# Two adaLN feed-forward layers on one core: the sort before everything, three blocks of items by gathers, eight places for block outputs, weights split two blocks later

## The reference, cut to what matters

```python
def _L0_cond_ref(x, weight, adapter_ids):        # x (64, 32, 512), weight (8, 512, 512)
    w = weight[adapter_ids]
    return jnp.einsum('bsi,boi->bso', x, w)

h  = _L0_cond_ref(x, L0_cond_weight, itok_B_3_7)
x  = x + (h @ kernel + bias + delta_lora(h, gate) + h @ A_shared.T @ B_shared.T)
c  = gated_ffn_with_lora(x, itok_B_2_6)          # 1376 wide, silu(gate) * up, down
x  = x + (c @ W.T + b + routed_lora(c))          # the best of four ranks per token
```

## Time and profile before

| | us |
|---|---|
| median of 3 runs (709.83 to 710.42) | 710.22 |
| the profiled execution | 711.87 |
| its span | 709.9 |
| TensorE busy | 682.0 (96%) |
| TensorE weight loads busy | 567.9 (80%) |
| VectorE busy | 312.5 (44%) |
| ScalarE busy | 281.5 (40%) |
| POOL busy | 346.0 (49%) |

### The profile page before, as it was taken

The page is one execution under the profiler, slowest core; times in us unless marked ns, Lnnn a source line. Parts: engine busy times, 40 slices in busy tenths (PEclk is TensorE's granted clock), DMA queues, the critical chain, the costliest instruction groups (busy, mean ns, idle before and its releaser), DMA issues. The chain is left out here.

```text
span 709.9 us, 11120 instructions
## 1 busy us (share of the span) xinstructions
PE 682.0 (96%) x3388; PEld 567.9 (80%) x3388; DVE 312.5 (44%) x719; ACT 281.5 (40%) x606; POOL 346.0 (49%) x266
## 2 busy tenths in 40 slices
PE   5799999998999999999999999999999999989997
PEld 3678788886788888888888888888888888867775
DVE  3788677646522223622222642142462223244664
ACT  2675542213543333543333554343454433343210
POOL 0034400231788765587766488776558777300000
PEclk9999999999999999999999999999999999999999
DMA  8963561121245336345334335433434434100112
GB/s 301 372 251 138 190 223 60 37 76 46 87 158 172 112 106 238 102 141 154 123 119 145 97 116 164 143 113 102 153 110 141 148 113 132 51 1 0 60 63 116
DMA packets 32210, 91.80 MB, mean 129 GB/s; under 512 B 5312, under 2 KB 5440, under 8 KB 30624
## 3 DMA queue, kind: packets, MB, share of 16 engines
q1 hardware_dynamic: 21936, 61.05, 25.5%
q0 software_dynamic: 10080, 30.16, 12.8%
q10 hardware_dynamic: 144, 0.00, 0.0%
HBM read 81.23 MB, written 9.96 MB: 128 GB/s over the span
## 5 line engine op out<-in xcount | busy, mean ns | idle before, releaser
L570 POOL TENSOR_TENSOR gu_lo<-gu_raw,gu_hi 128x1024 fp32r<-128x1024 f32 x44 | 113.2, 2572 | 101.7 <-ACT gu_hi L649 101.6
L1242 DVE TENSOR_TENSOR act_f<-psU,silu 128x512 f32<-128x512 f32 x44 | 30.4, 692 | 181.5 <-ACT silu L809 181.5
L601 POOL DMA_INDIRECT ab<-in_ab,idx_tab x88 | 85.9, 976 | 20.8 <-issue 17.3
L809 ACT ACTIVATE silu<-psG 128x512 f32<-128x512 f32 x44 | 26.2, 596 | 147.5 <-PE psG L1360 147.4
L1353 PE MATMUL psG<-x_hi,gu_hi 128*128 128x512 f32 x176 | 72.3, 411 | 1.2 <-ACT silu L809 1.2
L1353 PE MATMUL psD<-act_hi,dn_hi 128*128 128x512 f32 x176 | 69.0, 392 | 0.0
L1354 PE MATMUL psD<-act_lo,dn_hi 128*128 128x512 f32 x176 | 69.0, 392 | 0.0
L1355 PE MATMUL psG<-x_hi,gu_lo 128*128 128x512 f32 x176 | 68.9, 392 | 0.0
L1353 PE MATMUL psU<-x_hi,gu_hi 128*128 128x512 f32 x176 | 68.9, 391 | 0.0
L1354 PE MATMUL psG<-x_lo,gu_hi 128*128 128x512 f32 x176 | 68.6, 390 | 0.0
L1355 PE MATMUL psD<-act_hi,dn_lo 128*128 128x512 f32 x176 | 68.6, 390 | 0.0
(11 more groups left out here) (324 smaller groups left out, 1613.3 us busy)
## 6 DMA issues: line engine op xcount, KB each, us to landing
gu_raw<-in_gu SPq DMA_DIRECT2D x44, 512.0 KB, 3.5
dn_raw<-in_dn SPq DMA_DIRECT2D x44, 256.0 KB, 4.2
cond_w_raw<-in_cond_w SPq DMA_DIRECT2D x8, 1024.0 KB, 6.9
x_all<-in_x_t SPq DMA_DIRECT2D x4, 1024.0 KB, 10.5
tok<-h_scratch SPq DMA_DIRECT2D x4, 1024.0 KB, 5.5
out_t<-x_all SPq DMA_DIRECT2D x16, 256.0 KB, 2.1
ab<-in_ab,idx_tab POOLq DMA_INDIRECT x88, 3.8
kraw<-in_kern SPq DMA_DIRECT2D x1, 1024.0 KB, 11.9
```

Of the source, the lines that this page charges most:

```text
L570: pool.tensor_tensor(dst, x, hi, ALU.subtract).then_inc(s, 1)
L601: pool.indirect_dma_start(ab[:, par, g, :], None, a["ab"], bass.IndirectOffsetOnAxis(idx_tab[:, NGT * t + g, fc:fc + 1], 0)).then_inc(S[f" ...
L809: act.activation(silu[:], psG[:], ACT.Silu).then_inc(S["silu_s"], 1)
L1242: dve.tensor_tensor(act_f[:], psU[:], silu[:], ALU.mult).then_inc(S["act_f_s"], 1)
```

## The change

The sort's table is cut in three and its first part (64 rows of the columns that the sort needs, 115 KB) is loaded first, on ACT's queue, and the rest of the early part behind `ids1`, also there. `shared` is loaded three times, to 96 partitions, so that hi and lo parts stand above each other: the fold is one product of 96 rows per quarter instead of three of 32, and moves behind the products of `perm`; VectorE's split of it moves behind `blk_w`. VectorE makes `idx_x`, rows of x for blocks 0 to 2, and POOL gathers them from HBM into the first three places of `h0`; TensorE transposes them (`turn_x`: 0 ahead of block 0, 1 inside it, 2 behind it), and ScalarE and VectorE split them out of PSUM (`high_xg`, `low_xg`). Only x(0) and x(1) are loaded before the first weight; x(2) and x(3) wait for `xg_sent`, and weights 1 and 2 follow. Weight 1 is split at b = 0, weight k at b = 2(k - 1), and weights 3 to 7 are loaded when `c_ps` reaches b - 4 of their split; `kraw` goes behind weight 4. Blocks 4 to 7 are evicted to four more places (`h0_far`, in the last slot of `w_hi`). VectorE's loop over the blocks changes as ScalarE's does, and `scatter_rows` stands ahead of `low_w0(0)`. The diff, cut to its core:

```diff
 CONST_W = {
-    "ident": P, "adapter_no": N_ADP, "adapter_eighth": N_COND, "before": ITEMS, "ones": P, "fours": ITEMS // BI,
-    "slot_no": SLOTS, "delta": RANK0, "item_no": P, "dummy": SLOTS, "quadrant": BI, "row_in_item": 1,
-    "own_group": GROUPS, "heads": ITEMS,
+    "adapter_eighth": N_COND, "before": ITEMS, "ones": P, "fours": ITEMS // BI, "slot_no": SLOTS, "item_no": P,
+    "adapter_no": N_ADP,
+    "ident": P, "quadrant": BI, "row_in_item": 1, "own_group": GROUPS, "heads": ITEMS, "dummy": SLOTS, "delta": RANK0,
...
+        h0_far = sb("h0_far", [P, RING, D], F32, at=w_at - slot_bytes)
+        X_BANK = (psX, psG, psT)
...
+        SPLIT_AT = {2 * (k - 1): k for k in range(1, N_COND)}
...
+        def is_far(b):
+            return RING <= b < 2 * RING
+        def spot(b):
+            return (h0_far if is_far(b) else h0)[:, b % RING, :]
+        def spot_free(eng, b):
+            if b >= 2 * RING:
+                eng.wait_ge(S[f"c_st{b % RING}"], 16 * (b // RING - 1))
...
@@ block.sync
             sp.dma_start(ids0[:], a["ids0"]).then_inc(S["ids0_in"], 16)
-            sp.dma_start(const[:, 0:CONST_EARLY], a["const"][:, 0:CONST_EARLY]).then_inc(S["const_in"], 16)
-            sp.dma_start(sh[:], a["shared"]).then_inc(S["shared_in"], 16)
-            for t in range(NTB):
+            for k in range(3):
+                sp.dma_start(sh[k * RANK0:k * RANK0 + RANK0], a["shared"]).then_inc(S["shared_in"], 16)
+            def load_x(t):
                 sp.dma_start(x_all[:, :, tokens_of(t)], a["x_t"][t].rearrange("p (c n) -> p c n", c=C)
                              ).then_inc(S["x_all_in"], 16)
+            load_x(0)
+            load_x(1)
             sp.wait_ge(S["order_ready"], 1)
-            for k in range(3):
-                load_w(k)
-            sp.dma_start(kraw[:], a["kern"]).then_inc(S["kraw_in"], 16)
-            sp.dma_start(gate_v[:], a["gate"]).then_inc(S["gate_in"], 16)
+            load_w(0)
+            sp.wait_ge(S["xg_sent"], 1)
+            load_x(2)
+            load_x(3)
+            load_w(1)
+            load_w(2)
             sp.wait_ge(S["kern_ps"], C)
             sp.wait_ge(S["blk_ready"], 1)
             sp.wait_ge(S["idx_ready"], 1)
-            for k in range(3, N_COND):
-                sp.wait_ge(S["w_hi_s"], split_w(k - 3))
-                load_w(k)
+            sp.wait_ge(S["xg_ps"], AHEAD)
+            for b, k in SPLIT_AT.items():
+                if k > 2:
+                    multiplied(sp, b - 4)
+                    load_w(k)
+                if k == 4:
+                    sp.dma_start(kraw[:], a["kern"]).then_inc(S["kraw_in"], 16)
+                    sp.dma_start(gate_v[:], a["gate"]).then_inc(S["gate_in"], 16)
...
@@ block.gpsimd
+            pool.wait_ge(S["idx_x_ready"], 1)
+            for b in range(AHEAD):
+                pool.indirect_dma_start(h0[:, b, :], None, a["x"], bass.IndirectOffsetOnAxis(idx_x[:, b:b + 1], 0)
+                                        ).then_inc(S[f"xg_in{b}"], 16)
+                if b == 1:
+                    pool.tensor_copy(sent[:], idx_x[:]).then_inc(S["xg_sent"], 1)
             pool.wait_ge(S["idx_ready"], 1)
...
@@ block.scalar
+            act.dma_start(const[0:ITEMS, 0:CONST_SORT], a["const"][0:ITEMS, 0:CONST_SORT]).then_inc(S["const_in"], 16)
             act.dma_start(ids1[:], a["ids1"]).then_inc(S["ids1_in"], 16)
+            act.dma_start(const[:, CONST_SORT:CONST_EARLY], a["const"][:, CONST_SORT:CONST_EARLY]
+                          ).then_inc(S["ends_in"], 16)
+            act.wait_ge(S["shared_in"], 48)
+            high(sh_r[:], sh[:], S["sh_hi_s"])
+            def high_xg(b):
+                act.wait_ge(S["xg_ps"], b + 1)
+                high(xs_hi[:, b].rearrange("p c j n -> p (c j n)"), X_BANK[b][:], S["xs_hi"], BI)
             folded(0)
             folded(1)
+            act.wait_ge(S["w_in0"], 16)
+            high_w0(0)
+            high_xg(0)
+            for c in range(1, C):
+                high_w0(c)
+            folded(2)
+            high_xg(1)
+            folded(3)
+            high_xg(2)
             act.wait_ge(S["item_ready"], 1)
-            cols = item_cols(act, 0), item_cols(act, 1)
-            folded(2)
-            folded(3)
             act.wait_ge(S["x_all_in"], 16 * NTB)
-            high_xs(0, cols[0])
-            high_xs(1, cols[1])
-            act.wait_ge(S["w_in0"], 16)
-            for c in range(C):
-                high(w_hi[:, 0, c * D:c * D + D], w_raw[:, 0, c * D:c * D + D], S["w_hi_s"])
-            high_xs(2)
-            high_w(1)
             for b in range(NBLK):
...
-                if b % W_EVERY == 0 and b // W_EVERY + 2 < N_COND:
-                    high_w(b // W_EVERY + 2)
+                if b in SPLIT_AT:
+                    high_w(SPLIT_AT[b])
...
@@ block.vector
+            then(dve.tensor_tensor(sel_g[:], psT[:, 0:AHEAD * BI].rearrange("p (b j) -> p b j", j=BI),
+                                   cst("quadrant").unsqueeze(1).broadcast_to([P, AHEAD, BI]), ALU.mult))
+            then(dve.tensor_reduce(row_x[:], sel_g[:], AX.X, ALU.add))
+            dve.tensor_scalar(idx_x[:], row_x[:], float(ITEM_T), cst("row_in_item"), ALU.mult, ALU.add
+                              ).then_inc(S["idx_x_ready"], 1)
+            def low_xg(b):
+                dve.wait_ge(S["xs_hi"], BI * (b + 1))
+                flat = [v[:, b].rearrange("p c j n -> p (c j n)") for v in (xs_hi, xs_lo)]
+                dve.tensor_tensor(flat[1], X_BANK[b][:], flat[0], ALU.subtract).then_inc(S["xs_lo"], BI)
+            scatter_rows()
+            low_w0(0)
+            low_xg(0)
+            for c in range(1, C):
+                low_w0(c)
+            low_xg(1)
+            low_xg(2)
+            keep_counts()
...
@@ block.tensor
+            pe.wait_ge(S["sh_lo_s"], 2)
+            for c in range(C):
+                pe.matmul(psD[:, c, :], sh_r[:, 0, c * P:c * P + P], sh_r[:, 1, :], start=True, stop=True
+                          ).then_inc(S["kern_ps"], 1)
+            def turn_x(b):
+                pe.wait_ge(S[f"xg_in{b}"], 16)
+                if b == 2:
+                    pe.wait_ge(S["idx_ready"], 1)
+                for c in range(C):
+                    mm = pe.transpose(X_BANK[b][:, c * P:c * P + P], h0[:, b, c * P:c * P + P], ident)
+                mm.then_inc(S["xg_ps"], 1)
...
                     mm = pe.matmul(ps, xh, w[1], start=False, stop=c == C - 1)
+                    if b == 0 and c == 1:
+                        turn_x(1)
                 mm.then_inc(S["c_ps"], 1)
             pe.wait_ge(S["blk_ready"], 1)
             e = adapter(0)
+            turn_x(0)
             for b in range(NBLK):
                 after = adapter(b + 1) if b + 1 < NBLK else None
                 cond(b, e)
+                if b == 0:
+                    turn_x(2)
                 e = after
```

More of the change, by code:

```diff
@@ L278, in two_layers @@
         sh_at = w_at + 6 * slot_bytes
-        sh = sb("shared", [RANK0, 2, D], F32, at=sh_at)
-        sh_lo = sb("shared_lo", [RANK0, 2, D], F32R, at=sh_at)
-        sh_hi = sb("shared_hi", [RANK0, 2, D], F32R, at=sh_at + 4 * 2 * D)
+        sh = sb("shared", [3 * RANK0, 2, D], F32, at=sh_at)
+        sh_r = sb("shared_r", [3 * RANK0, 2, D], F32R, at=sh_at + 4 * 2 * D)
         top["at"] = w_at + 5 * slot_bytes
@@ L289, in two_layers @@
         own = sb("own", [ITEMS, N_COND], F32)
+        sel_g = sb("sel_g", [P, AHEAD, BI], F32)
+        row_x = sb("row_x", [P, AHEAD], F32)
+        idx_x = sb("idx_x", [P, AHEAD], U32)
+        sent = sb("sent", [P, AHEAD], U32)
         slot = sb("slot", [ITEMS, 1], F32)
@@ L382, in two_layers @@
         a_rows = a["ab"].rearrange("n (k d) -> (n k) d", k=3)
-        names = """ids0_in const_in shared_in gate_in small_in ids1_in lora_a_in lora_b_in kraw_in late_in
+        names = """ids0_in const_in ends_in shared_in idx_x_ready xg_sent xg_in0 xg_in1 xg_in2 xg_ps gate_in small_in ids1_in lora_a_in lora_b_in kraw_in late_in
             w_in0 w_in1 w_in2 w_in3 w_in4 w_in5 w_in6 w_in7
@@ L389, in two_layers @@
             kern_ps kfold_s kern_f kern_hi kern_lo aeff_ps beff_ps aeff_done beff_even beff_odd
-            w_hi_s w_lo_s xs_hi xs_lo c_ps c_out0 c_out1 c_st0 c_st1 c_st2 c_st3
+            w_hi_s w_lo_s xs_hi xs_lo c_ps c_out0 c_out1 c_st0 c_st1 c_st2 c_st3 c_far0 c_far1 c_far2 c_far3
             wf_hi_s wf_lo_s
@@ L922, in _ @@
             dve.tensor_reduce(item_w[:], own_w[:], AX.X, ALU.add).then_inc(S["item_w_s"], 1)
+            dve.wait_ge(S["ids1_in"], 16)
+            dve.tensor_copy(ids1f[:], ids1[:]).then_inc(S["ids1_f"], 1)
+            dve.wait_ge(S["ends_in"], 16)
+            dve.wait_ge(S["sort_ps2"], 1)
+            then(dve.tensor_tensor(sel_g[:], psT[:, 0:AHEAD * BI].rearrange("p (b j) -> p b j", j=BI),
[3 more added lines that the diff above has]
+                              ).then_inc(S["idx_x_ready"], 1)
+            dve.wait_ge(S["sort_ps3"], 1)
```

(38 more changed lines are left out.)

63 lines of the change are left out of this document (32 added, 31 removed).

## The result

The changed kernel takes 712.81 us at the median (711.54 to 714.99, 7 runs), the kernel before 710.06 in the same comparison (708.6 to 710.42, 7 runs): ratio 1.0044, interval 1.0028 to 1.0060, 3.1 us slower (2.75 by the medians). A second set gave 1.0047 (1.0029 to 1.0065). I had forecast 709.8 with a range of 707.0 to 711.8.

A forecast was written before the change was run, and what follows sets the result against it. TensorE, busy for 96% of the 709.9 us span, was taken as the bound. The terms -3.1 + 1.4 - 0.1 + 0.4 + 1.7 + 0 - 0.7 gave -0.4 us, median 709.8, range 707.0 to 711.8.

The forecast's parts named there:

- The start: Before phase 1's first product: earlier sort and weights let TensorE begin at 19.0 instead of 22.12, -3.1 us.
- Transposes: Phase 1, block 0 and behind it: turn_x(1) and turn_x(2) add 1.4 us; clock's lower level with the start moved, -0.1.
- Blocks 3 to 5: After block 0: the ScalarE and VectorE run of splits and evictions ends later than TensorE wants it, +0.4 us.
- The later split: At b = 12: low_w(7) beside kraw on VectorE makes xs_lo(16) late, so block 16 starts late, +1.7 us.
- Eight places, loads by progress: Block outputs and weight loads in phase 1: more places and loads released by c_ps change nothing, both 0.
- The end of phase 1: TensorE's wait for gsel_lo: with TensorE later from block 16, about 0.4 of 1.06 us is left, -0.7 us.
- Rival B: Slower, +2.4 us (712.6): low_w(7) and kraw stop TensorE 2.5 us before block 16, start at 20.2; chance 0.14.

The follow-up runs named there:

- e3: Changed kernel with the load of lora_b waiting for 18 blocks instead of 16: 713.07 us, ratio 1.0031 to the kernel before.
- e2: Changed kernel with only the addition to kraw moved from b = 12 to b = 14: 710.06 us, ratio 0.9995 to the kernel before.
- e1: The changed kernel run again unaltered, for its spread and a second trace: 712.9 us, ratio 1.0047 to the kernel before.
- e7: Kernel before with every weight split two blocks later, and no other part of the change: 714.68 us, ratio 1.0056 to the kernel before.
- e4: Changed kernel with kraw at b = 14 and lora_b after 18 blocks: 708.3 us, ratio 0.9975 to the kernel before.
- e10: Kernel before with lora_b after 18 blocks alone: 709.79 us, ratio 0.9991 to the kernel before.
- e11: Changed kernel with kraw at b = 14 and lora_b after 18 blocks, run once more: 709.16 us, ratio 0.9987 to the kernel before.
- e6: Changed kernel with four places for the block outputs instead of eight: 714.0 us, ratio 1.0050 to the kernel before.
- e8: Changed kernel with x(2) and x(3) issued right behind the first weight, not held back: 715.09 us, ratio 1.0073 to the kernel before.
- e9: Changed kernel with kraw at b = 14, lora_b after 18 blocks and x(1) also held behind the second gather: 708.97 us, ratio 0.9994.
- e5: Changed kernel with the old order of splits, weight 1 ahead of the loop, weight k at b = 2(k - 2): 713.31 us, ratio 1.0041.

## Why the prediction was wrong, by its steps

The sum was off by 1.5 us in the traces (-0.4 forecast, +1.06 measured), the median by 3.0 (709.8 forecast, 712.8 measured). The other 1.5 is a step of its own: I moved the median by the sum, as if both traces lay equally far from their medians, and they did not.

**The start** (-3.1, bounds -4.2 and -1.9; measured -4.8, in e3 only -2.2). The end of the sort (`w_order`, the first weight's issue) was right within 0.2 us, the weights' landing was forecast 2.8 us too late. I had carried over the landing of x(0) from the earlier trace rows, 7.6 us after issue; the shortest of the four now took 6.0, and the weights 5.1. I then charged the gathers to the weights, where the weights were through first and the start hung on the gather. What I missed altogether is that this start is not a number but a spread. In the eight traces that keep x(1), x(2) and x(3) as in the change it is 17.23 to 19.95, 2.8 us behind the landing of the first gather, and where the gather was latest (e2, e3) x(0) and the first weight were late too.

**Transposes** (+1.4 - 0.1): +1.2, right in the trace shown, but in part by luck: there TensorE kept its lower level for 6.8 us from the first product, in e1 for 3.6, and block 0 and its transpose cost only 0.1 more than before. **Blocks 3 to 5** (+0.4, bounds 0 and 1.0): +0.86 from block 3 to 4, and +1.2 in e1, where x was late as well. Right in kind.

**The later split** (+1.7, bounds 0 and 2.5): +2.19. The mechanism is as written, by its rows, and e2 and e7 show it from both sides. Of the 0.5 that the term was short, 0.3 is in blocks 13 to 15, which ran in 8.20 us where the trace before has 8.48, so that block 16 was wanted sooner; the rest goes with ScalarE's hi of weight 7: I wrote that nothing is waited for there, and VectorE waited 1.09 us (in its row). Not in the sum at all was that a stop of 2.1 us can drop TensorE to its lower level for 3 us, 1.6 us more in block 16, in half the traces.

**"Eight places, loads by progress: 0."** This is the step that failed. I looked for who waits for a scatter today, and found one, at block 18. I did not carry my own delay forward: the same 2.3 us of VectorE work put off evacuate(13), with it the scatter of block 13, and kern_f, behind which SP issues lora_a, so that lora_a and lora_b, which waits for 16 blocks, go out together at 67.0 and 67.4. Scatter 13 then goes out at 67.9 behind 2 MB and takes 10.3 us; in the trace before lora_a was issued at 67.35, the scatter at 68.20, lora_b at 69.69, and it took 7.1. Measured in place of the 0: +1.41 before block 20 (+0.88 in e1), gone when lora_b is held (e3, e4), and made by the later split alone (e7).

**The end of phase 1** (-0.7): +0.41. I had TensorE late and the others on time; but evacuate(17) and (18) were late by the same scatters, so the two did not catch up. Where no eviction waits for a scatter (e3, e4, e10, e11), 0.2 us of that wait is left. This term was wrong by 1.1 us, through the same step.

Rival B had the sign and the place. It put its 2.4 us into a start at 20.2 and a longer stop, and neither was so in the trace shown. With the terms as measured the sum is +1.06 against the first trace of the kernel before and 2.0 to 2.3 against the second; where the remaining 0.8 to 1.1 us to the median's 3.1 lies stays open. The traces show several things that vary by as much in either kernel: the landing of the gather, the moment at which TensorE's pace rises in block 0 (it takes 4.61 or 5.28 us before, 5.4 to 6.5 after), the small stops before blocks 8 and 12, and the rest behind phase 1 (622.9 to 624.3). How often each happens in unprofiled runs I can't show.

## What to carry to other kernels

When a fixed piece of work is moved to a later iteration, list what else is pinned to that iteration: where one piece of 2.3 us left a slack of 0.9, a second one did not fit, and moving one of them (kraw, together with the load of lora_b) cost nothing elsewhere (e4). Then carry the delay forward through every queue it touches; its second effect (a scatter that now falls behind two loads) was two thirds as large as the first in one trace and 0.4 of it in another. An early start bought with a small gather gained from holding the big loads back while it flies, and even so it came at a time that varied by 2.7 us. And see where a trace stands among its kernel's runs before moving a median by it: here that was half of the miss.

## What the runs showed of the hardware that I had not expected

The first 1 MB load in SP's queue landed 6.7 to 7.6 us after issue in the four traces of the kernel before and its variants, and 5.9 to 7.6 us in the ten with the changed order of small loads. The two ranges overlap, so the difference between the first two traces (7.6 and 6.0) is not shown to come of the order. The first indirect DMA on POOL took 1.54 us to issue and the next two 0.95 and 0.97. A TensorE that had been busy since its first product, but for stops of at most 0.6 us, fell to 0.43 us per product (granted clock 0.50) within 0.3 to 1.1 us of the end of a stop of 1.96 to 2.08 us in three traces (e3, e6, e8), and did not after stops of 2.03, 2.08 and 1.78 us in three others; nor did it after one of 1.73 us before block 4 (e9). After the stop of 3.96 us in e5 it did. In the first microseconds of phase 1 the granted clock reads 1.00 although the products start 0.43 us apart (from 17.4 to 23.4 in the trace shown); there the level is read from the spacing.
